# A recommender's last layers: a bias that enters PSUM as a product, and a layer cut into two column halves

## The reference, cut to what matters

```python
x = relu(x @ Wt1 + bt1)     # 479 -> 1024
x = relu(x @ Wt2 + bt2)     # 1024 -> 1024
x = relu(x @ Wt3 + bt3)     # 1024 -> 512
x = relu(x @ Wt4 + bt4)     # 512 -> 256
return sigmoid(x @ Wo + bo) # 256 -> 1
```

## Time and profile before

| what | value |
|---|---|
| median of 3 runs | 273.59 us (272.95 to 273.87) |
| the profiled execution | 272.63 us |
| its span, first to last instruction | 270.8 us |
| mean granted TensorE clock | 0.824 of full speed |
| PE matmul busy | 191.6 us, 71% of the span |
| PE weight load busy | 133.0 us, 49% |
| DVE busy | 71.3 us, 26% |
| ACT busy | 59.0 us, 22% |

### The profile page before, as it was taken

One profiled execution on the slowest core, in us unless ns is written; L12 is line 12 of the kernel. 1 busy time (PEld: TensorE's weight loads), 2 busy tenths in 40 slices (PEclk: granted clock), 3 DMA queues, 4 the chain that ended last, 5 costly groups with the idle time before them and its releaser, 6 DMA issues.

```text
span 270.8 us, 3791 instructions
## 1 busy us (share of the span) xinstructions
PE 191.6 (71%) x1657; PEld 133.0 (49%) x1657; DVE 71.3 (26%) x131; ACT 59.0 (22%) x97; POOL 100.0 (37%) x111
## 2 busy tenths in 40 slices
PE   5996201012946389695958695959879999899994
PEld 2333001002523257474835463837656678677872
DVE  3040001100642275631201232120225321253222
ACT  3661110010451362530101020100112111111001
POOL 5777777724472606444364445260600000000000
PEclk9998755555695658989895599795999999999999
DMA  5988859621020201101020101020100000000000
GB/s 145 361 251 258 255 188 290 205 87 41 19 61 16 52 0 33 39 21 41 10 61 19 39 22 48 5 56 0 41 10 2 0 2 2 0 2 0 2 0 0
DMA packets 8082, 18.18 MB, mean 67 GB/s; under 512 B 2309, under 2 KB 3593, under 8 KB 7938
## 3 DMA queue, kind: packets, MB, share of 16 engines
q1 hardware_dynamic: 4738, 11.12, 12.7%
q0 software_dynamic: 3328, 6.82, 9.8%
HBM read 17.93 MB, written 0.00 MB: 66 GB/s over the span
## 4 chain that ended last, share of the span: by engine, by line
PE 63%; issue 23%; DVE 6%; another core or an unknown queue 4%; ACT 2%; DMA 1%; SPq 0%; DVEq 0%; ACTq 0%
PE mp L442 19%; PE gp L377 9%; PE mp L463 9%; PE mp L413 7%; PE gp L367 4%; PE tp L421 4%; PE mp L333 3%; PE mp L325 3%; PE mp L348 2%; DVE xb L689 2%; PE gp L389 1%; DVE w2l L661 1%; PE mp L475 1%; ACT xth L555 1%
## 5 line engine op out<-in xcount | busy, mean ns | idle before, releaser
L312 POOL DMA_INDIRECT rows<-in_emb,row_of x104 | 99.1, 953 | 95.2 <-PE gp L367 60.5
L377 PE MATMUL gp<-zt 128*32 128x27 f32 x1024 | 25.9, 205 | 57.9 <-issue 52.5
L377 PEld LDWEIGHTS gp<-zt 128*32 128x32 f32 x1024 | 18.5, 119 | 70.8 <-issue 70.8
L544 ACT COPY zt<-gp 128x512 f32<-128x512 f32 x16 | 9.4, 586 | 99.7 <-PE gp L367 67.3
L442 PE MATMUL mp<-w2h,a1l 128*128 128x512 f32 x64 | 29.3, 458 | 1.2 <-DVE a1l L705 0.6
L442 PE MATMUL mp<-w2l,a1h 128*128 128x512 f32 x64 | 28.7, 448 | 0.0
L442 PE MATMUL mp<-w2h,a1h 128*128 128x512 f32 x64 | 28.5, 445 | 0.0
L367 PE MATMUL gp<-ident,rows 128*128 128x128 f32 x104 | 19.4, 310 | 4.9 <-ACT zt L544 4.9
L367 PEld LDWEIGHTS gp<-ident,rows 128*128 128x128 f32 x104 | 15.3, 163 | 12.1 <-issue 9.0
L711 DVE TENSOR_TENSOR raw<-mp,bc 128x512 f32<-128x512 f32 x8 | 5.5, 691 | 44.5 <-PE mp L442 44.5
L442 PEld LDWEIGHTS mp<-w2h,a1l 128*128 128x128 f32 x64 | 13.8, 215 | 5.0 <-DVE a1l L705 1.3
(11 more groups left out here) (71 smaller groups left out, 208.3 us busy)
## 6 DMA issues: line engine op xcount, KB each, us to landing
w<-in_wt SPq DMA_DIRECT2D x13, 512.0 KB, 5.7
rows<-in_emb,row_of POOLq DMA_INDIRECT x104
w<-in_wt SPq DMA_DIRECT2D x3, 468.0 KB
bc<-in_rows SPq DMA_DIRECT2D x1, 1024.0 KB
wd_sb<-in_wd SPq DMA_DIRECT2D x1, 512.0 KB
w1d<-in_wt SPq DMA_DIRECT2D x1, 512.0 KB
bt<-in_rows SPq DMA_DIRECT2D x1, 512.0 KB
wdf_sb<-in_wdf SPq DMA_DIRECT2D x1, 128.0 KB
```

The lines of the kernel that those rows point to most:

```text
L312: pool.indirect_dma_start(out=rows[:, n % RING, :], out_offset=None, in_=emb.rearrange("c v e -> (c v) e"), in_offset=bass.IndirectOffsetO ...
L377: last = pe.matmul(gp[SQ * q:SQ * (q + 1), g // 16, c:c + NZ], zt[:, g % 16, q, :], zt[:, g % 16, q, 0:NZ], start=True, stop=True)
L544: sc.copy(zt_features(j, 0, 16), transposed(g, 0, 16)).then_inc(zt_act, 1)
```

## The change

Two edits. First, layer 4's bias: TensorE multiplies a column of ones, `ones` [1, 128], by the row of bt4 as the first product of layer 4's accumulation, and DVE's addition of the bias with its wait goes, for all four tiles. The next tile's layer 1 now waits for `logits_ready` where it waited for `z4_ready`. Second, the last tile's layer 3: instead of 24 matmuls with 512 columns there are 48 with 256, in two PSUM banks that the features used; the loop goes over the halves of the rows first (`half`), then over the halves of the columns (`h`). The transposes of layer 3's result move into layer 3 and layer 4.

```diff
+LAST_TURN = 7
-        z4 = sb("z4", [P, 2, TOP[4]])
+        z4 = sb("z4", [P, TOP[4]])
+        ones = sb("ones", [1, P])
@@ layer_1
                     if n == PRODUCTS_1 // 2:
-                        at_least(pe, z4_ready, t)
+                        at_least(pe, logits_ready, t)
@@ PE, last tile
+            def last_layer_3(t):
+                for half in range(2):
+                    for h in range(2):
+                        for n in range(PRODUCTS_3 // 2):
+                            if half == 1 and h == 0 and n == 0:
+                                turn(t, 3)
+                            if half == 1 and h == 1 and n == LAST_TURN:
+                                last_turn(t, 0)
+                            k, part = 4 * half + n // 3, n % 3
+                            if h == 0 and n == 0:
+                                pe.wait_ge(a2_hi, 2 * t + half + 1)
+                            if h == 0 and n == 2:
+                                pe.wait_ge(a2_lo, 2 * t + half + 1)
+                            a, w = ((a2h, w3h), (a2h, w3l), (a2l, w3h))[part]
+                            last = pe.matmul(gp[:, 2 + h, 0:TOP[3] // 2], a[:, k, :], w[:, k, h * 2 * P:(h + 1) * 2 * P],
+                                             start=(half == 0 and n == 0), stop=(half == 1 and n == PRODUCTS_3 // 2 - 1))
+                        if half == 1:
+                            last.then_inc(l3_ready, 1)
+            def last_turn(t, h):
+                pe.wait_ge(raw_ready, TURNS * t + 4 + h + 1)
+                for c in range(2):
+                    last = pe.transpose(tp[:, h, c * P:(c + 1) * P], raw[:, 0, (2 * h + c) * P:(2 * h + c + 1) * P], ident[:])
+                last.then_inc(turned, 1)
             def layer_4(t):
                 if t == 0:
                     pe.wait_ge(w4_in, 16)
+                    pe.wait_ge(rows_sem, 16)
+                    pe.wait_ge(zeroed, 3)
+                pe.matmul(mp[:, 1, 0:TOP[4]], ones[:], bc[0:1, ROW4:ROW4 + TOP[4]], start=True, stop=False)
                 for k in range(M3):
                     if t < TILES - 1 and k == 0:
                         pe.wait_ge(a3_ready, t + 1)
+                    if t == TILES - 1 and k == 2:
+                        last_turn(t, 1)
                     if t == TILES - 1 and k % 2 == 0:
                         pe.wait_ge(a3_ready, t + 1 + k // 2)
-                    last = pe.matmul(mp[:, 1, 0:TOP[4]], a3[:, k, :], w4[:, k, :], start=(k == 0), stop=(k == M3 - 1))
+                    last = pe.matmul(mp[:, 1, 0:TOP[4]], a3[:, k, :], w4[:, k, :], start=False, stop=(k == M3 - 1))
                 last.then_inc(l4_ready, 1)
...
-            layer_3(t)
-            for h in range(2):
-                pe.wait_ge(raw_ready, TURNS * t + 4 + h + 1)
-                for c in range(2):
-                    last = pe.transpose(tp[:, h, c * P:(c + 1) * P], raw[:, 0, (2 * h + c) * P:(2 * h + c + 1) * P], ident[:])
-                last.then_inc(turned, 1)
+            last_layer_3(t)
             layer_4(t)
@@ DVE
+            ve.memset(ones[:], 1.0).then_inc(zeroed, 1)
             def last_layers(t):
                 ve.wait_ge(l4_ready, t + 1)
-                ve.tensor_tensor(z4[:, 0, :], mp[:, 1, 0:TOP[4]], bc[:, ROW4:ROW4 + TOP[4]], ALU.add).then_inc(z4_ready, 1)
-                ve.wait_ge(z4_ready, t + 1)
-                ve.scalar_tensor_tensor(out=z4[:, 1, :], in0=z4[:, 0, :], scalar=0.0, in1=bc[:, ROWO:ROWO + TOP[4]], op0=ALU.max,
+                ve.scalar_tensor_tensor(out=z4[:], in0=mp[:, 1, 0:TOP[4]], scalar=0.0, in1=bc[:, ROWO:ROWO + TOP[4]], op0=ALU.max,
                                         op1=ALU.mult, accum_out=logits[:, t:t + 1]).then_inc(logits_ready, 1)
@@ DVE, last tile
-            ve.wait_ge(l3_ready, t + 1)
             for h in range(2):
-                ve.tensor_tensor(raw[:, 0, 2 * h * P:2 * (h + 1) * P], mp[:, 0, 2 * h * P:2 * (h + 1) * P],
+                ve.wait_ge(l3_ready, t + h + 1)
+                ve.tensor_tensor(raw[:, 0, 2 * h * P:2 * (h + 1) * P], gp[:, 2 + h, 0:TOP[3] // 2],
                                  bc[:, ROW3 + 2 * h * P:ROW3 + 2 * (h + 1) * P], ALU.add).then_inc(raw_ready, 1)
             last_layers(t)
```

## The result

The change makes the kernel slower: 276.65 us median (275.83 to 277.79, 4 runs) against 273.73 (272.95 to 273.88), ratio 1.0127, interval 1.0095 to 1.0160. Two later comparisons with the same kernel gave 1.0091 (1.0056 to 1.0127) and 1.0113 (1.0071 to 1.0156). As ratios that is 2.5 to 3.5 us, as differences of the medians 2.3 to 2.9, where +1.3 was forecast. The direction and the first pause came as predicted; the size did not. One of e5's twelve runs, 275.11 us, counts as a slow one and is left out of e5's ratio.

What follows compares the result with a forecast made beforehand. The prediction took a chain of PE work as the bound, DVE and ACT counting only where PE waits. Last tile +1.1 and other tiles +0.2 gave +1.3 us, 274.9 us (+0.5%) by the median, range 273.5 to 276.7.

Steps and rivals of the forecast that it cites:

- the first pause: Last tile's layer 3, behind turn(t, 3): PE stands still 1.42 us in two pieces, waiting for ACT, then DVE.
- The price of a 256-column product: Last tile's layer 3: each 256-column product, p, takes 0.122 us, with 0.110 and 0.19 kept as ends.
- step 5: Last tile's layer 4: bias product is two matmuls, 0.43 us; the second half's conversion is not hidden.
- The last tile: Last tile becomes 1.10 us longer: columns +0.24, pause +1.42, DVE's addition -0.46, way from layer 3 to DVE -0.09.
- DVE's addition: Removing DVE's layer 4 bias addition saves 0.46 us in the last tile and nothing in tiles 0 to 2.
- Tiles 0 to 2: Bias product at the tile boundaries: +0.05 us at each later one, 0.10 at tiles 0 and 1, together +0.2.
- a move of more than 0.5 ahead of the last tile: Sign: the prediction is wrong if the time before the last tile moves by more than 0.5 us.
- The load-bound price: Rival: the weight load sets the price per 256-column product, 0.19 us each, total 278.0 us; chance 0.10 for all forms.
- no pause: Rival: products behind turn(t, 3) find their inputs, so the change does nothing, 273.5 us; chance 0.07.
- the clock in favour: Rival: a 1.2 GHz stretch at 168 or 182 to 189 us goes, 273.2 or 271.5 us; chance 0.11.
- a further stretch at 1.2 GHz: Rival: one more slow-clock stretch, for instance behind the last tile's new pause, costs 1.7 us, 276.6 us; chance 0.12.
- The mild form of the load-bound price: Rival: 256-column products at 0.15 us each, +2.6 us, 276.2 us; within the 0.10 for all load-bound forms.

Runs made afterwards that it cites:

- e5: Kernel before with last tile only changed: column halves, early turn(t, 3), second transposes after layer 4's first chunk, 128-row bias product after its second; ratio to before 0.9959.
- e3: Changed kernel with turn(t, 3), the transposes, moved to after eight products of the first column half's first row half; ratio to before 1.0077.
- e11: Same kernel as e3, timed a second time in a later comparison; ratio to before 1.0070.
- e12: The changed kernel unedited, timed again beside e9, e10 and e11; ratio to before 1.0113.
- e4: Changed kernel with the bias product made over 128 rows (ones matrix of 1/128) instead of one row; ratio to before 1.0090.
- e9: Same kernel as e1, timed a second time in a later comparison; ratio to before 1.0069.
- e1: Kernel before with only the one-row bias product in all four tiles, layer 3 left at 512 columns; ratio to before 1.0101.
- e6: Changed kernel with the edits of e3 and e4 together, bias product over 128 rows in all tiles; ratio to before 0.9991.
- e7: The changed kernel unedited, timed again in the comparison with e5 and e6; ratio to before 1.0091.
- e2: Kernel before with only the column halves of the last tile's layer 3, DVE still adding layer 4's bias; ratio to before 1.0078.
- e10: Same kernel as e2, timed a second time in a later comparison; ratio to before 1.0068.

## Why the prediction was wrong in size

**The price of a 256-column product.** Taken 0.122, measured 0.117: the whole distance scales with the columns. 46 x 0.005 = 0.23 too much was charged. It would have been 0.86 instead of 1.10 for the last tile.

**The pause.** Predicted 1.42 and the third product 2.10 behind the transposes. Its load started 2.01 behind, plus 0.11: 2.12. Right, and e3 takes it away by moving one line: 1.35 us, in e11 against e12 1.45.

**Layer 4's bias product, step 5, "0.43, whatever its single row of ones holds".** It costs nearly twice that: 0.82 in the last tile, and 0.62 at the warm boundaries, where only the seam behind it costs. Between this product of one row and its neighbours of 128, neither weight load starts ahead; over 128 rows (e4) both do, and the cost is 0.43. The Trainium skill ("TensorEngine Tiling (Array Packing)", "Key Properties") says that changing the tiling mode, not just the tile, drains TensorE. It gives no price and does not say that a product of one row is such a change. The trace and e4 agree with that reading, 0.39 us for the two seams, but no run here tells a drain from another reason for which the loads wait. I weighed a rule on row groups for products that all have 128 rows, and did not ask it of the only product that has one. At 1.2 GHz the prediction's price was up to 0.85; from the first load of the ones to layer 4's first load pass 1.15:

```profile
152.35 0.50 PEld L472 LDWEIGHTS mp<-bc,ones 1*128 1x128 f32 x2
...
153.50 3.06 PEld L478 LDWEIGHTS mp<-w,a 128*128 128x128 f32 x8 [0.65 <-issue]
```

These lines are of e9, at the boundary of tiles 0 and 1; e12 has 1.15 there too.

**The last tile.** +1.32 (11.46 against 10.14), predicted +1.10: less 0.23 for the columns, plus 0.39 for the seams, and 0.06 in smaller distances.

**DVE's addition.** Worth nothing in tiles 0 to 2, as said. In the last tile e1 shows that it is worth only 0.05 if the one-row product goes ahead of layer 4 (10.09 against 10.14). Of what goes back, 0.19 is the seam (0.62 from load to load, not 0.43).

**One remark on a price.** The prediction says that N / 2.4 + 2.5 ns agrees with layer 4's matmuls, 0.216 apart. They have 256 columns, for which that formula gives 0.109; it agrees only if each of the two matmuls of a float32 product counts as 512 columns, which the prediction does not say. The 0.216 itself is the trace's, and so is what is built on it.

**Tiles 0 to 2, "together +0.2, between 0.1 and 0.4".** This is the step that failed: the bias product was taken as nearly covered at every boundary. The last tile's layer 3 starts at 260.04 instead of 257.86, 2.2 later, and the prediction had itself named a move of more than 0.5 ahead of the last tile as a sign of being wrong. By the ratios of the three comparisons, less the last tile's +1.3 to +1.4, it is 1.1 to 2.2. In its parts:

- The two warm boundaries cost 0.24 each, not 0.05, by the seam of 0.19 (e4, e6: 0.05).
- The boundary of tiles 0 and 1 costs 0.9 in the trace (3.52 against 2.62), where I took 0.10. Two things went together. I had put the transposes behind layer 4 at 2.4 GHz, 0.11 apart, because the clock rose at 155 in the trace of before; it stayed at 1.2 GHz to 157, with the transposes 0.21 apart. And the cover had been used up, so that the slower clock counts in full. How much of this comes differs from run to run: the same changed kernel takes 3.52, 2.62 and 3.79 here (e7's granted clock from 155 to 157 is 0.86, not 0.50). Over the nine traces with a bias product in tiles 0 to 2 this boundary takes 2.6 to 4.2, mean 3.6; over the five without, 2.6 to 3.5, mean 2.9. So 0.7 on average, with a spread within either group that is larger than that; it can't be read from one trace.
- The rest is 0.8 in that trace: tile 1 between its two boundaries takes 0.95 more (47.14 against 46.19, its granted clock 0.86 in the mean against 0.89), and 0.2 is won ahead of it. Over the same traces, xth of the last tile starts at 242.7 in the mean against 240.8, 1.9 later, of which the boundaries make about 1.1. Of the other 0.8, 0.5 to 0.6 lies in tile 1 and 0.3 ahead of the boundary of tiles 0 and 1, where xb waits for the grams, which stand ahead of the first bias product. Whether it belongs to the bias product, through the clock, or to chance stays open. e6 speaks against it for a product over 128 rows; for the one-row product no run shows it either way. The granted clock of all runs leans for it, not clearly: in the mean 0.808 to 0.812 for the kernels with the one-row product, 0.814 to 0.817 for the kernel before, 0.811 to 0.815 for e2, e4, e5, e6 and e10. And e2 and e10 lie 0.8 to 1.0 over their steps although they have no such product.

**The rivals.** The load-bound price, no pause and the clock in favour did not come. The one that I gave 0.12 (a further stretch at 1.2 GHz, 276.6) names the right time by luck: it adds one more slow stretch of 1.7 us to +1.3, while the traces show 0.4 to 0.5 at the warm boundaries and 0.39 in the last tile that no clock explains. Part of its mechanism, more time at 1.2 GHz, is seen in the changed kernel's trace at boundary 0/1 and in tile 1. The mild form of the load-bound price, 276.2, comes near the time as well, with a price of 0.15 per product where 0.117 was measured. Faster was never near.

## What to carry to other kernels

When work is reordered on an engine that runs its list in order, look at what stands directly behind a step whose outcome it needs: the same 48 products lose 1.35 us or nothing by the place of four transposes. A bias as a one-row product is not a free ride on an accumulation: make it with as many rows as its neighbours have (e4), and put it where the engine waits anyway (e5). Price it at the slower clock wherever the cover is thin, and take an average over several traces for a stage in which the clock changes.

## What the runs showed of the hardware

- A fp32r product starts 0.117 us behind the one before with 256 columns and 0.234 with 512, at 2.4 GHz: no fixed part per product, although at 1.2 GHz 512 columns take 0.43, less than twice as much.
- At a distance of 0.117 each product's own weight load is still hidden: behind the pause, two loads start 0.11 apart (264.14 and 264.25) and the products then keep 0.117.
- The load of a one-row product begins 0.21 us behind the start of the matmul before it, and the next load of 128 rows 0.30 behind the start of the product's second matmul; between products of equal rows both distances are nothing. Over 128 rows the same product costs 0.43 in all against 0.82. At 1.2 GHz the one-row product takes 1.15 from load to load (e9), at 2.4 GHz 0.62.
